# Softmax normalisation and phase wrapping on GpSimd, a split closing sum and new instruction orders in a one-core token-fusion kernel

## The chip, the cores and the metric

One Trainium2 chip, one of its cores. The time is the device time of one launch in microseconds (us); the median of several runs counts. The engines are PE (TensorE, matrix products, with its weight loads PEld), DVE (VectorE), ACT (ScalarE), POOL (GpSimd) and SP (SyncE, which issues most transfers). Each has its own queue of instructions and works through it in order; they wait for each other by semaphores only.

## The reference

Sixteen images and sixteen texts go through three layers. All arithmetic is fp32.

```python
# 1. tokens of an image: 2x2 convolution of stride 2 -> 144 tokens of 64, one attention without heads
feat = conv(x, conv_w) + conv_b                        # reshaped to (16, 144, 64)
Q, K, V = feat @ wq.T + bq, feat @ wk.T + bk, feat @ wv.T + bv
h = softmax(Q @ K.T / 8) @ V @ wo.T + bo
h = concatenate([h, txt], axis=1)                      # (16, 272, 64)
# 2. a phase memory on layernorm(h), added to h
n = layernorm(h)
pos = (cumsum(v1 * cos(p)) * cos(p) + cumsum(v1 * sin(p)) * sin(p)) / sqrt(t)   # p = base_phases, v1 = n @ Wvp + bvp
kp, qp = pi * tanh(tanh(n @ Wk1 + bk1) @ Wk2 + bk2), pi * tanh(tanh(n @ Wq1 + bq1) @ Wq2 + bq2)
content = (causal memory of cos/sin(kp) with n @ Wvc + bvc, read by cos/sin(qp)) / sqrt(32 t)
g = softmax(relu(n @ Wg1 + bg1) @ Wg2 + bg2)
h = h + n + (layernorm(g0 * pos + g1 * content) * ln_g + ln_b) @ Wo + bo
# 3. eight experts on layernorm(h), the best two of each token, added to h
n = layernorm(h)
w = softmax over the two largest of n @ Wg + bg, zero elsewhere
h = h + sum_e w[e] * (gelu(n @ W1[e] + b1[e]) @ W2[e] + b2[e])
```

## The kernel before

**Tiles.** The 64 features lie on the partitions, two images at a time (64 + 64 = 128), so sixteen images are eight pairs of 272 columns each. Layers 1 and 2 run over pairs (0 to 7); everything that goes token by token (layer norms, gates, routing, experts) runs over five groups of 3, 4, 4, 3 and 3 windows of 128 columns (`GW`, groups 0 to 4).

**Stages.** A stage is a name with an index, such as `exps:3`. For a pair: `taps` (DVE, the convolution, three sets of pairs), `qk` (PE, then `qkv` on DVE and `keys` on ACT copy the result out), `scores` (PE, then the row maximum on DVE), `exps` (ACT, four exponentials with their row sums, L585), `probs_n` (DVE, reciprocal and one multiplication, L817 and L819), `probs_t` (PE transposes, ACT copies), `mix` (PE, ACT). Then `h0_t` and `ln1_stats`/`ln1_norm` for a group (DVE; the power -1/2 comes from POOL, L484, the `root` helper), `residual` (POOL, L503 and L506), and for a pair `hidden`, `phases`, `phase_abs`, `trig`, `memory`, `recall`, `content`, and `streams` (DVE running sum, then POOL L511 and L512). A group goes on with `combine`, `ln2_stats`, `norm_s`, `attn_out`, `ln3_stats`, `ln3_norm`, `xn2_t`, `route`, `weights_t`, `wide` (transfers that spread the routing weights), sixteen `expert` products (PE, gelu on ACT, L697), eight `expert_out` products (PE L1236; DVE multiplies by the weight, L952; POOL adds up, L523) and `finish` (PE transposes the sum back, L1208, DVE adds it to `res`, L958, SP stores).

**Once only.** `base` takes the base phases into (-pi, pi] with six DVE instructions on 128x272 (L786 to L791), then ACT takes sines (L563 to L566), which needs another table than the exponentials, and POOL multiplies. `ln2_w` folds the layer norm's scale and bias into a weight: it waits for the transfer of `attw` (L657, L658 on ACT; L1176, L1177 on PE).

**What sets the order.** Each engine runs through a list of stages written out in `PLAN`; a stage waits for its inputs and for its PSUM bank, and all that stands behind it on that engine waits too. `BANKS` gives each stage its bank. `spare:n` in PE's list puts n matmuls on a matrix of ones into the bank that the next stage takes, behind that bank's last reader:

```python
                for _ in range(spare.pop() if spare else 0):
                    pe.matmul(ps[:, bank, 0:128], ones[:, 0:128], ones[:, 0:128], start=True, stop=True)
```

Of the kernel before, what the change touches and what calls it, by code (L numbers as in the profile page):

```python
# [139 lines left out]
phases:2 content:3 content:4 mix_gate:2 recall:0 gate_z:2 h0_t:4 memory:1 hidden:3 hidden:4 memory:2 phases:3  # L140
phases:4 recall:1 xn_t:3 xn_t:4 combine:0 content:5 mix_gate:3 memory:3 content:6 norm_s:0 content:7
mix_gate:4 attn_out:0 hidden:5 hidden:6 hidden:7 phases:5 phases:6 gate_z:3 gate_z:4 memory:4 values:2
phases:7 recall:2 recall:3 memory:5 memory:6 recall:4 recall:5 xn2_t:0 values:3 values:4 route:0 expert:0
memory:7 expert:1 logit_t:0 values:5 expert:2 expert:3 expert:4 combine:1 expert_out:0 expert_out:1 recall:6
combine:2 recall:7 norm_s:1 expert:5 weights_t:0 attn_out:1 norm_s:2 expert:6 expert_out:2 expert:7 attn_out:2
expert:8 expert_out:3 expert:9 values:6 values:7 expert:10 expert_out:4 xn2_t:1 expert:11 route:1 expert:12
expert:13 logit_t:1 expert_out:5 expert_out:6 expert:14 expert:15 spare:1 expert:16 expert_out:7 weights_t:1
combine:3 xn2_t:2 expert:17 route:2 expert:18 expert:19 norm_s:3 logit_t:2 expert:20 expert:21 expert:22
expert:23 attn_out:3 expert_out:8 expert_out:9 expert_out:10 expert_out:11 weights_t:2 expert:24 expert:25
# [1176 lines left out]
```

## Time and profile before

| | |
|---|---|
| median of 3 runs | 248.57 us (248.51 to 248.88) |
| the profiled execution | 249.06 us, of which 247.3 us from its first to its last instruction |
| granted TensorE clock, mean | 0.979 of full speed |
| busy share of the span | PE 91%, DVE 68%, ACT 60%, PEld 52%, POOL 41% |
| chain that ended last | PE 54%, DVE 23%, issue 9%, ACT 5%, SP's queue 4%, POOL 2% |

The busy shares are means over stages with different limits; a stretch is read by the engine that is busy nearly all of it. The chain is followed back from the last instruction, at each step to what released it.

### The profile page before, as it was taken

To read this page: it belongs to the slowest core of one execution; us is meant where nothing else is said; L and a number is where in the kernel's file an instruction comes from. 1 tells how busy PE (TensorE), PEld (TensorE's weight loads), DVE (VectorE), ACT (ScalarE), POOL (GpSimd) and SP (SyncE) were. 2 spreads that over 40 slices of the span, in tenths; PEclk is the share of its full clock that TensorE was granted. 3 is DMA by queue.
4 is the path that set the end of the run, shared out by engine and by line. 5 is a ranking of instruction groups with operands and counts; after the bars stand their busy time and mean duration, and the time that the engine had idled before them with its cause. 6 is when DMAs were issued, how large, how long until landed. Compare 5 with 4: busy or idle time off the path is not lost.

```text
span 247.3 us, 4625 instructions
## 1 busy us (share of the span) xinstructions
PE 226.0 (91%) x1546; PEld 128.0 (52%) x1546; DVE 167.1 (68%) x485; ACT 148.0 (60%) x300; POOL 102.1 (41%) x93
## 2 busy tenths in 40 slices
PE   7689799698889999999978999998999999999991
PEld 5578577475776765644324433542433445445440
DVE  2779587999999999999999791849023553213121
ACT  4677978885674775344546806592843655673640
POOL 3000233778852529156865253415146043333333
PEclk9959999999999999999999999999999999999997
DMA  7671000000000000026000933920900025601001
GB/s 187 140 252 67 0 3 0 0 3 0 5 0 3 0 3 0 3 71 189 1 0 19 243 86 96 243 42 7 248 6 0 0 48 144 158 1 32 0 3 32
DMA packets 15239, 14.42 MB, mean 58 GB/s; under 512 B 8528, under 2 KB 13680, under 8 KB 15088
## 3 DMA queue, kind: packets, MB, share of 16 engines
q1 hardware_dynamic: 14640, 13.66, 21.8%
q10 hardware_dynamic: 576, 0.47, 0.7%
q8 instruction: 13, 0.21, 0.4%
q14 instruction: 10, 0.08, 0.1%
HBM read 12.87 MB, written 1.25 MB: 57 GB/s over the span
## 4 chain that ended last, share of the span: by engine, by line
PE 54%; DVE 23%; issue 9%; ACT 5%; SPq 4%; POOL 2%; DMA 1%; POOLq 0%; ACTq 0%; DVEq 0%
PE ps L1223 22%; PE ps L1236 17%; ACT arena L585 3%; DVE stat L747 3%; DVE trig L862 2%; DVE scaled L952 2%; DVE y L852 2%; PE ps L1169 2%; DVE xn L771 1%; DVE k L780 1%; DVE vc L842 1%; SPq L411 1%; PE ps L973 1%; DMA attw<-in_attw 1%; PE ps L1011 1%
## 5 line engine op out<-in xcount | busy, mean ns | idle before, releaser
L697 ACT ACTIVATE arena<-ps,cols 128x768 f32<-128x768 f32 (+1 forms) x80 | 73.5, 990 | 30.6 <-PE ps L1223 26.3
L1223 PE MATMUL ps<-xt,w 64*128 64x384 f32 (+1 forms) x320 | 66.2, 544 | 0.2 <-DVE mem L872 0.2
L523 POOL TENSOR_TENSOR acc<-acc,scaled 128x384 f32<-128x384 f32 (+1 forms) x35 | 40.3, 1153 | 55.7 <-DVE scaled L952 54.8
L1236 PE MATMUL ps<-arena,w 128*64 128x384 f32 (+1 forms) x320 | 62.1, 534 | 0.5 <-DVE scaled L952 0.5
L952 DVE SCALAR_TENSOR_TENSOR scaled<-ps,b_col,wide 128x384 f32<-128x384 f32 (+1 forms) x35 | 23.2, 669 | 48.2 <-PE ps L1236 48.1
L484 POOL TENSOR_TENSOR rstd<-vare,minus_half 128x6 f32<-128x6 f32 (+1 forms) x15 | 24.8, 1652 | 46.3 <-DVE vare L756 46.1
L1223 PEld LDWEIGHTS ps<-xt,w 64*128 64x128 f32 x320 | 28.9, 186 | 26.3 <-issue 10.8
L1236 PEld LDWEIGHTS ps<-arena,w 128*64 128x64 f32 x320 | 21.5, 136 | 37.0 <-issue 29.2
L511 POOL TENSOR_TENSOR cum<-cum,turn_n 128x544 f32<-128x544 f32 x8 | 11.2, 1398 | 9.6 <-DVE cum L856 9.6
L721 DVE SCALAR_TENSOR_TENSOR arena<-arena,cols 128x108 f32<-128x108 f32 (+1 forms) x36 | 9.2, 312 | 5.3 <-ACT arena L550 5.1
L585 ACT ACTIVATE arena<-ps,negmax 72x144 f32<-72x144 f32 x32 | 11.6, 375 | 1.0 <-DVE negmax L812 1.0
L611 ACT ACTIVATE xt<-ps 128x256 f32<-128x256 f32 (+1 forms) x20 | 6.0, 350 | 10.1 <-PE ps L1064 10.1
L856 DVE TENSOR_TENSOR_SCAN cum<-ones,y 128x544 f32<-128x544 f32 x8 | 11.7, 1456 | 0.3
L492 POOL TENSOR_TENSOR turn_n<-turn_p,phase 128x544 f32<-128x544 f32 x1 | 1.3, 1333 | 24.1 <-ACT turn_p L566 24.1
L747 DVE BATCH_NORM_STATS2 stat<-res 128x6 f32<-128x64 f32 x68 | 9.5, 210 | 0.2
L973 PE MATMUL ps<-ones 128*128 128x128 f32 x28 | 4.5, 293 | 5.4 <-ACT arena L572 2.5
L1130 PE MATMUL ps<-trig 64*128 64x272 f32 (+2 forms) x96 | 8.5, 308 | 0.9 <-ACT trig L641 0.9
L1130 PEld LDWEIGHTS ps<-trig 64*128 64x128 f32 x96 | 7.8, 186 | 2.5 <-issue 1.3
L512 POOL TENSOR_TENSOR h0s<-cum 128x272 f32<-128x272 f32 x8 | 8.4, 1051 | 0.6
L872 DVE TENSOR_TENSOR mem<-ps,mask 128x864 f32<-128x864 f32 x8 | 8.3, 1043 | 0.2
L1141 PE MATMUL ps<-mem,vc 128*64 128x272 f32 (+2 forms) x96 | 7.6, 297 | 0.7 <-DVE mem L872 0.7
L771 DVE SCALAR_TENSOR_TENSOR xn<-xn,rstd 128x384 f32<-128x384 f32 (+1 forms) x10 | 8.1, 811 | 0.2
(158 smaller groups left out, 365.0 us busy)
## 6 DMA issues: line engine op xcount, KB each, us to landing
wide<-rows_of SPq DMA_DIRECT2D x24, 192.0 KB, 4.1
wide<-rows_of SPq DMA_DIRECT2D x16, 256.0 KB, 6.0
w<-in_w SPq DMA_DIRECT2D x1, 1024.0 KB, 5.2
out<-res SPq DMA_DIRECT2D x6, 96.0 KB, 1.9
h0s<-in_txt SPq DMA_DIRECT2D x1, 512.0 KB, 5.9
w<-in_w SPq DMA_DIRECT2D x1, 512.0 KB, 6.0
out<-res SPq DMA_DIRECT2D x4, 128.0 KB, 3.3
arena<-in_x_a SPq DMA_DIRECT2D x2, 144.0 KB, 3.6
```

The lines of the kernel that those rows point to most:

```text
L484: pool.tensor_tensor(rstd[:, kind, g % 2, 0:nb(g)], vare[:, kind, g % 2, 0:nb(g)], minus_half[:, 0:nb(g)], ALU.pow).then_inc(rstd_ok[kind], 1)
L511: link(pool.tensor_tensor(cum[:, i % 2, :, :], cum[:, i % 2, :, :], turn_n[:, :, :], ALU.mult))
L523: pool.tensor_tensor(acc[:, g % 2, 0:128 * GW[g]], acc[:, g % 2, 0:128 * GW[g]], scaled[:, i % 2, 0:128 * GW[g]], ALU.add).then_inc(S["acc ...
L585: ins = act.activation(probs[0:SC, i % 2, k, :], ps[0:SC, bank("scores", i) + k // 2, SI * (k % 2):SI * (k % 2) + SI], ACT.Exp, bias=negma ...
L697: act.activation(hidden_e[:, i % HIDDEN, 0:2 * n].rearrange("p (h t) -> p h t", h=2), ps[:, b:b + 2, 0:n], ACT.Gelu, bias=col("b1", 2 * e ...
L747: ins = dve.bn_stats(stat[:, g % 2, k, :], src[:, 64 * k:64 * k + 64])
L771: return dve.scalar_tensor_tensor(out=blocks(dst[:, 0:64 * n]), in0=blocks(dst[:, 0:64 * n]), scalar=8.0, in1=spread(rstd[:, kind, g % 2, ...
L856: dve.tensor_tensor_scan(cum[:, i % 2, :, :].rearrange("p k t -> p (k t)"), ones[:, :], y[:, i % 2, :, :].rearrange("p k t -> p (k t)"), 0 ...
L952: dve.scalar_tensor_tensor(out=total, in0=ps[:, bank("expert_out", i), 0:n], scalar=b2_col[:, e:e + 1], in1=wide[:, g % 2, e, 0:n], op0=AL ...
L1130: ins = pe.matmul(ps[:, bank("memory", i) + h, MOFF[k]:MOFF[k] + L - q], trig[r, 0, L * i + m:L * i + m + 128], trig[r, 1, L * i + q:L * i ...
L1223: ins = pe.matmul(ps[:, bank("expert", i) + h, 0:n], w1[r, c:c + 128], xt[r, GC[g]:GC[g] + n], start=True, stop=True)
L1236: ins = pe.matmul(ps[64 * h:64 * h + 64, bank("expert_out", i), 0:n], w2[:, 2 * (i % E) + j, :], hidden_e[:, (2 * i + j) % HIDDEN, n * h:n ...
```

## The change

Five edits and new lists:

1. `probs_n`: DVE keeps the reciprocal; the multiplication of 72x576 goes to POOL, in a stage of POOL's list, and PE's `probs_t` waits for it there.
2. `base`: the wrapping goes from DVE to POOL as a stage `reduce:0`, nine instructions for six, since each multiply-and-add becomes two. ACT's `base:0` stands early, ahead of `keys:2` and the first `exps`.
3. `spare`: three matmuls in one place, in bank 5, which no stage ahead of it uses, and without a wait; before, fourteen in five places.
4. `ln2_w` stands later on PE and ACT.
5. The last `expert_out` (index 39) is not added by POOL. DVE writes it in three pieces, and PE's `finish:4` turns back both the sum so far and the last piece into one bank (matmuls with the identity, the second adding to the first). ACT issues one of the last two stores. `attn_out` gets a buffer of its own (`ao` for `c2`).

```diff
+SPARE = [(3, 5)]
+CLOSING = (5, 2, 3)
...
-qk:0 qk:1 spare:3 scores:0 scores:1 ln2_w:0 qk:2 qk:3 val:0 probs_t:0 val:1 qk:4 scores:2 mix:0 val:2 qk:5
+qk:0 qk:1 spare:0 scores:0 scores:1 val:0 val:1 qk:2 qk:3 qk:4 ln2_w:0 probs_t:0 scores:2 probs_t:1 mix:0 qk:5
...
+                if stage == "probs_n":
+                    pool.wait_ge(S["rowinv"], i + 1)
+                    pool.tensor_tensor(probs[0:SC, i % 2, :, :], probs[0:SC, i % 2, :, :],
+                                       rinv[0:SC, i % 2, :].unsqueeze(2).to_broadcast([SC, 4, SI]), ALU.mult)\
+                        .then_inc(S["pnorm"], 1)
+                elif stage == "reduce":
+                    pool.wait_ge(ld["phase"], 16)
+                    raw = phase[:, 0, :]
+                    link(pool.tensor_scalar(turns[:, :], raw, float(1 / (2 * np.pi)), ROUND, ALU.mult, ALU.add))
+                    link(pool.tensor_scalar(turns[:, :], turns[:, :], ROUND, None, ALU.subtract))
+                    for part in (TWO_PI_1, TWO_PI_2, TWO_PI_3):
+                        link(pool.tensor_scalar(turn_n[:, 0, :], turns[:, :], part, None, ALU.mult))
+                        link(pool.tensor_tensor(raw, raw, turn_n[:, 0, :], ALU.subtract))
+                    pool.tensor_scalar(raw, raw, PI32, -PI32, ALU.min, ALU.max).then_inc(S["reduced"], 1)
...
-                elif stage == "expert_out" and i % E > 0:
+                elif stage == "expert_out" and 0 < i % E and i < E * NG - 1:
...
+            act.wait_ge(S["out_sb"], NG)
+            act.dma_start(*store_of(NG - 1, 1)).then_inc(S["stored"], 16)
...
+                    if i >= 2:
+                        dve.wait_ge(S["pnorm"], i - 1)
                     dve.reciprocal(rinv[0:SC, i % 2, :], rsum[0:SC, i % 2, :]).then_inc(S["rowinv"], 1)
-                    dve.wait_ge(S["rowinv"], i + 1)
-                    dve.tensor_tensor(probs[0:SC, i % 2, :, :], probs[0:SC, i % 2, :, :],
...
+                    if i == E * NG - 1:
+                        for w in range(GW[g]):
+                            c = slice(128 * w, 128 * w + 128)
+                            dve.scalar_tensor_tensor(out=total[:, c], in0=ps[:, bank("expert_out", i), c], scalar=b2_col[:, e:e + 1],
+                                                     in1=wide[:, g % 2, e, c], op0=ALU.add, op1=ALU.mult).then_inc(S["last_sb"], 1)
...
+                    if i == NG - 1:
+                        pe.wait_ge(S["acc_sb"], added(i, E - 2))
+                        last = (E * NG - 1) % 2
+                        for w in range(GW[i]):
+                            take(CLOSING[w], "out_sb", NG)
+                            pe.matmul(ps[:, CLOSING[w], 0:128], acc[:, i % 2, 128 * w:128 * w + 128], ident[:, :],
+                                      start=True, stop=False)
+                        for w in range(GW[i]):
+                            pe.wait_ge(S["last_sb"], w + 1)
+                            pe.matmul(ps[:, CLOSING[w], 0:128], scaled[:, last, 128 * w:128 * w + 128], ident[:, :],
+                                      start=False, stop=True).then_inc(S["last_mm"], 1)
```

Where the lists differ, three places matter for the prediction. In these rows a name is the tile written, then the tiles read, with the shape of the output; `arena` holds all of layer 1, `ps` is PSUM, `cols` and `rows` are parameters. First **ACT's queue in the opening**, from `keys:0` on, before:

```order
L572 ACTIVATE arena<-ps,cols 128x144 x2
L557 ACTIVATE wvo<-ps 128x128
L558 ACTIVATE bvo<-ps,cols 128x1
L657 ACTIVATE scaled_wo<-attw,cols 128x128
L658 ACTIVATE ln_b_w<-ones,cols 128x128
L585 ACTIVATE arena,rsum<-ps,negmax 72x144 x4
```

and now:

```order
L593 ACTIVATE arena<-ps,cols 128x144 x2
L578 ACTIVATE wvo<-ps 128x128
L579 ACTIVATE bvo<-ps,cols 128x1
L557 ACT_TABLE_LOAD
L584 ACTIVATE turn_p<-phase 128x272
L585 ACTIVATE turns<-phase 128x272
L587 ACTIVATE turn_p<-turns,cols 128x272
L593 ACTIVATE arena<-ps,cols 128x144
L557 ACT_TABLE_LOAD
L606 ACTIVATE arena,rsum<-ps,negmax 72x144 x4
L678 ACTIVATE scaled_wo<-attw,cols 128x128
```

The sines with their two table loads and `keys:2` now stand ahead of the first exponentials, and the norm fold behind them.

Second **POOL's queue in layer 1 and the start of layer 2** (`cum` is the running sum of `streams`, `rstd` the power -1/2), before:

```order
L492 TENSOR_TENSOR turn_n<-turn_p,phase 128x544
L484 TENSOR_TENSOR rstd<-vare,minus_half 128x6
L500 TENSOR_TENSOR out_row<-out_row,rows 128x64
L503 TENSOR_TENSOR res<-res,out_row 128x384
L506 TENSOR_TENSOR res<-res,xn 128x384
L484 TENSOR_TENSOR rstd<-vare,minus_half 128x8
L503 TENSOR_TENSOR res<-res,out_row 128x512
L506 TENSOR_TENSOR res<-res,xn 128x512
L484 TENSOR_TENSOR rstd<-vare,minus_half 128x8
```

and now, behind the nine instructions of `reduce:0`:

```order
L513 TENSOR_TENSOR turn_n<-turn_p,phase 128x544
L497 TENSOR_TENSOR arena<-arena,rinv 72x576 x4
L491 TENSOR_TENSOR rstd<-vare,minus_half 128x6
L521 TENSOR_TENSOR out_row<-out_row,rows 128x64
L524 TENSOR_TENSOR res<-res,out_row 128x384
L527 TENSOR_TENSOR res<-res,xn 128x384
L497 TENSOR_TENSOR arena<-arena,rinv 72x576 x2
L491 TENSOR_TENSOR rstd<-vare,minus_half 128x8
L497 TENSOR_TENSOR arena<-arena,rinv 72x576
L524 TENSOR_TENSOR res<-res,out_row 128x512
L527 TENSOR_TENSOR res<-res,xn 128x512
L497 TENSOR_TENSOR arena<-arena,rinv 72x576
```

The eight multiplications (L497) stand among the powers and the residual sums; the power for group 2 is the next row.

Third **PE's last rows**, before:

```order
L1236 MATMUL ps<-arena,w 64x384 x8
L1223 MATMUL ps<-xt,w 128x384 x10
L1236 MATMUL ps<-arena,w 64x384 x16
L1208 MATMUL ps<-ident,acc 128x128 x3
L218 UNCONDITIONAL_BRANCH
```

and now:

```order
L1278 MATMUL ps<-arena,w 64x384 x4
L1265 MATMUL ps<-xt,w 128x384 x10
L1278 MATMUL ps<-arena,w 64x384 x20
L1250 MATMUL ps<-ident,acc 128x128 x3
L1241 MATMUL ps<-ident,acc 128x128 x3
L1245 MATMUL ps<-ident,scaled 128x128 x3
L220 UNCONDITIONAL_BRANCH
```

`finish:3` (the first three on `acc`) has come to the end too, ahead of the six matmuls of `finish:4`.

## Rows read from the trace of the kernel before

**Rows 1.** Busy us by stretch: length, then PE, PEld, DVE, ACT, POOL, granted clock.

```profile
10.00:20.00 10.00, 8.06 (x54) 7.52 (x54) 7.56 (x24) 6.36 (x30) 0.00 (x0) 0.66 0.60 199
...
30.00:40.00 10.00, 8.41 (x81) 6.68 (x81) 6.92 (x22) 8.52 (x37) 4.20 (x4) 1.00 0.01 2
40.00:50.00 10.00, 7.94 (x86) 5.59 (x85) 9.51 (x38) 8.16 (x31) 5.61 (x4) 1.00 0.00 0
50.00:60.00 10.00, 9.22 (x90) 6.61 (x87) 9.82 (x23) 7.41 (x16) 7.51 (x6) 1.00 0.01 2
60.00:70.00 10.00, 8.23 (x97) 6.63 (x95) 9.79 (x24) 6.77 (x15) 8.17 (x7) 1.00 0.01 3
...
120.00:130.00 10.00, 8.13 (x44) 3.13 (x40) 9.52 (x23) 4.41 (x6) 7.84 (x6) 1.00 0.00 1
...
160.00:180.00 20.00, 19.12 (x92) 7.85 (x90) 9.77 (x36) 13.80 (x18) 5.54 (x4) 1.00 0.43 102
```

**Rows 2.** Timeline: start, duration in us, engine, line; brackets: idle before, its releaser.

```profile
9.79 2.01 DVE L721 SCALAR_TENSOR_TENSOR arena<-arena,cols 128x108 f32<-128x108 f32 x8
...
14.05 0.40 ACT L657 ACTIVATE scaled_wo<-attw,cols 128x128 f32<-128x128 f32 x1 [2.79 <-DMA attw<-in_attw]
...
14.65 0.36 ACT L585 ACTIVATE arena<-ps,negmax 72x144 f32<-72x144 f32 x1
...
40.15 0.62 ACT L605 ACTIVATE res<-ps 128x512 f32<-128x512 f32 x1
```

**Rows 3.** Timeline of ACT around the sines of the base phases.

```profile
24.78 1.28 ACT L536 ACT_TABLE_LOAD   x1
...
26.86 0.52 ACT L566 ACTIVATE turn_p<-turns,cols 128x272 f32<-128x272 f32 x1
...
28.20 1.28 ACT L536 ACT_TABLE_LOAD   x1
```

**Rows 4.** Groups by line and shape: count, busy us, mean ns, idle before.

```profile
L511 POOL TENSOR_TENSOR cum<-cum,turn_n 128x544 f32<-128x544 f32 x8 | 11.2, 1398 | 9.6 <-DVE cum L856 9.6
...
L512 POOL TENSOR_TENSOR h0s<-cum 128x272 f32<-128x272 f32 x8 | 8.4, 1051 | 0.6
...
L819 DVE TENSOR_TENSOR arena<-arena,rinv 72x576 f32<-72x576 f32 x8 | 7.3, 912 | 0.3
...
L721 DVE SCALAR_TENSOR_TENSOR arena<-arena,cols 128x108 f32<-128x108 f32 x24 | 6.4, 324 | 0.8 <-ACT arena L550 0.7
...
L789 DVE SCALAR_TENSOR_TENSOR phase<-turns,phase 128x272 f32<-128x272 f32 x3 | 1.3, 442 | 0.1
```

**Rows 5.** Transfers: issues, KB each, median us from issue to landing.

```profile
out<-res SPq DMA_DIRECT2D x6, 96.0 KB, 1.9
...
phase<-in_phase ACTq DMA_DIRECT2D x1, 272.0 KB, 4.2
```

**Rows 6.** Timeline of POOL and DVE in the end of layer 1.

```profile
45.61 1.27 POOL L503 TENSOR_TENSOR res<-res,out_row 128x512 f32<-128x512 f32 x1 [0.81 <-DVE xn L771]
...
45.78 1.72 DVE L819 TENSOR_TENSOR arena<-arena,rinv 72x576 f32<-72x576 f32 x1
...
50.01 0.75 DVE L819 TENSOR_TENSOR arena<-arena,rinv 72x576 f32<-72x576 f32 x1
```

**Rows 7.** Timeline of PE at the routing weights of group 1.

```profile
130.25 0.27 PE L1197 MATMUL ps<-ident,wsp 128*64 128x128 f32 x1 [1.22 <-DVE wsp L933]
```

**Rows 8.** Timeline of the end, behind the last expert product.

```profile
241.55 0.62 DVE L952 SCALAR_TENSOR_TENSOR scaled<-ps,b_col,wide 128x384 f32<-128x384 f32 x1 [0.67 <-PE ps L1236]
242.25 0.99 POOL L523 TENSOR_TENSOR acc<-acc,scaled 128x384 f32<-128x384 f32 x1 [0.29 <-DVE scaled L952]
...
243.39 0.52 PE L1208 MATMUL ps<-ident,acc 128*128 128x128 f32 x3 [1.88 <-POOL acc L523]
243.94 0.56 DVE L958 TENSOR_TENSOR res<-ps,res 128x384 f32<-128x384 f32 x1 [1.77 <-PE ps L1208]
244.53 0.90 SPq L455 DMA_DIRECT2D out<-res  x2
```

More of the change, by code:

```diff
@@ L140 @@
[L140 to L149, printed above, removed]
@@ L150 @@
-expert:26 expert:27 expert_out:12 expert_out:13 xn2_t:3 finish:0 combine:4 route:3 expert:28 expert:29
-norm_s:4 logit_t:3 expert:30 expert:31 expert:32 expert:33 expert:34 expert:35 expert:36 attn_out:4
-weights_t:3 expert_out:14 expert_out:15 expert_out:16 xn2_t:4 expert:37 expert:38 expert:39 expert:40
-expert:41 expert:42 expert:43 expert_out:17 expert_out:18 expert_out:19 expert_out:20 expert_out:21 route:4
-expert:44 expert:45 expert:46 expert:47 expert:48 expert:49 logit_t:4 finish:1 expert_out:22 expert_out:23
@@ new lines @@
+mix_gate:2 memory:0 gate_z:2 phases:2 phases:3 h0_t:4 recall:0 memory:1 hidden:4 memory:2 memory:3 phases:4
+recall:1 xn_t:3 values:2 xn_t:4 combine:0 mix_gate:3 content:5 content:6 content:7 mix_gate:4 hidden:5
+hidden:6 gate_z:3 norm_s:0 gate_z:4 phases:5 phases:6 attn_out:0 hidden:7 recall:2 recall:3 phases:7 memory:4
+memory:5 memory:6 values:3 values:4 recall:4 memory:7 xn2_t:0 recall:5 route:0 expert:0 expert:1 logit_t:0
+expert:2 recall:6 combine:1 expert:3 expert:4 expert_out:0 expert_out:1 norm_s:1 values:5 weights_t:0 expert:5
@@ new lines @@
+attn_out:1 expert:6 expert:7 expert_out:2 expert_out:3 expert:8 combine:2 recall:7 expert:9 expert:10 values:6
+expert:11 norm_s:2 xn2_t:1 expert_out:4 route:1 expert:12 logit_t:1 attn_out:2 expert_out:5 expert:13
+expert:14 combine:3 expert_out:6 expert:15 expert:16 weights_t:1 values:7 expert_out:7 norm_s:3 expert:17
+attn_out:3 expert:18 expert:19 expert:20 expert_out:8 expert_out:9 xn2_t:2 expert:21 expert:22 expert:23
+expert_out:10 expert_out:11 route:2 expert:24 expert:25 expert:26 logit_t:2 expert:27 expert_out:12
@@ new lines @@
+expert_out:13 xn2_t:3 weights_t:2 finish:0 combine:4 route:3 expert:28 expert:29 norm_s:4 logit_t:3 expert:30
+expert:31 expert:32 expert:33 expert:34 expert:35 expert:36 expert:37 weights_t:3 attn_out:4 expert_out:14
+expert_out:15 expert_out:16 expert_out:17 expert_out:18 xn2_t:4 expert:38 expert:39 expert:40 expert:41
+expert:42 expert:43 expert_out:19 expert_out:20 expert_out:21 route:4 expert:44 expert:45 expert:46 expert:47
+expert:48 expert:49 logit_t:4 expert_out:22 expert_out:23 expert_out:24 weights_t:4 finish:1 expert:50
@@ L178 @@
[L178 to L179 removed]
+taps:0 taps:1 taps:2 taps:3 qkv:0 qkv:1 taps:4 taps:5 scores:0 scores:1 qkv:2 taps:6 qkv:3 taps:7 qkv:4 taps:8
+gate_w:0 probs_n:0 probs_n:1 scores:2 qkv:5 probs_n:2 scores:3 qkv:6 probs_n:3 ln1_stats:0 scores:4 ln1_norm:0
+qkv:7 scores:5 probs_n:4 probs_n:5 ln1_stats:1 scores:6 gate_p:0 scores:7 content:0 ln1_norm:1 probs_n:6
+streams:0 probs_n:7 ln1_stats:2 phase_abs:0 content:1 gate_p:1 ln1_norm:2 content:2 streams:1 ln1_stats:3
@@ L180 @@
+expert_out:26 expert_out:27 expert_out:28 expert_out:29 expert_out:30 finish:2 expert_out:31 expert_out:32
+expert_out:33 expert_out:34 expert_out:35 expert_out:36 expert_out:37 expert_out:38 expert_out:39 finish:3
+finish:4
 """),
     "act": order("""
-tap0:0 fold_t:0 tap0:1 tap0:2 keys:0 keys:1 fold:0 ln2_w:0 exps:0 ln2_wc:0 exps:1 keys:2 keys:3 probs_t:0
-val:0 val:1 keys:4 mix:0 val:2 exps:2 keys:5 probs_t:1 base:0 mix:1 probs_t:2 exps:3 h0_t:0 keys:6 mix:2 val:3
-val:4 val:5 val:6 probs_t:3 exps:4 mix:3 val:7 xn_t:0 exps:5 probs_t:4 gate_h:0 keys:7 h0_t:1 mix:4 probs_t:5
@@ L971, in take @@
                 reader[bank] = (S[read_out], count)
-                for _ in range(spare.pop() if spare else 0):
-                    pe.matmul(ps[:, bank, 0:128], ones[:, 0:128], ones[:, 0:128], start=True, stop=True)
             wq, wk, wo, wv = (tokw[:, 128 * k:128 * k + 128] for k in range(4))
@@ L997, in _ @@
                 if stage == "spare":
-                    spare.append(i)
+                    n, b = SPARE[i]
+                    if b in reader:
+                        pe.wait_ge(*reader[b])
+                    for _ in range(n):
+                        pe.matmul(ps[:, b, 0:128], ones[:, 0:128], ones[:, 0:128], start=True, stop=True)
                 elif stage == "qk":
```

183 lines of the change are left out of this document (91 added, 92 removed), and 8 rows, old and new, of the table BANKS.

## Prediction

> **What bounds the kernel now.** I read the busy time by stretch first [rows 1]. From 40 us on DVE is busy 9.5 to 9.8 of every 10 us, so it bounds layer 2. In the stretch 30 to 40 it is busy only 6.9 of 10 and ACT 8.5: there ACT and the way round between the engines bound layer 1. In 160 to 180 PE is busy 19.1 of 20 while DVE is at half: PE bounds the experts. POOL is nobody's bound by its share of the span, but in 60 to 70 it is busy 8.2 of 10 beside a full DVE. Then I read the opening [rows 2, 3]: ACT waits 2.79 us for `attw` and starts its first exponentials at 14.65; later it spends 24.78 to 29.48 on two table loads of 1.28 and three sines, a `mix` and a `probs_t` copy among them. The end [rows 8] is a chain without overlap: last product, DVE, POOL, PE, DVE, stores.
>
> So a microsecond counts in full where DVE is saturated, where ACT is (up to `h0_t:1`, which ends at 40.15 + 0.62 = 40.77), where PE idles among the experts, and in the closing chain.
>
> **Opening and layer 1 (edits 1 to 4).** Removed from ACT between 24.8 and 29.5: two table loads and the sines, which fill 26.06 to 27.38 [rows 3], so 2 x 1.28 + 1.32 = 3.9 us of a nearly full engine. They move ahead of the first `exps`, into the time in which ACT waited for `attw`, which waits no more there. What they cost is set by POOL's nine instructions of `reduce:0`. The phases land at about 2.2 + 4.2 = 6.4 [rows 5], the issue being the last of ACT's four. No row shows POOL at this work with one operand. From below I take DVE's own 0.44 for 128x272, from above POOL's 1.05 for two operands of that size, blocked times included [rows 4]: 4.0 to 9.5 us in all. Two thirds read one operand, so I take 0.75 each, 6.8 us: done at 13.2. ACT comes to the table load at 14.05 - 2.79 = 11.3 [rows 2] and has it by 12.6. The sines then end at 13.2 + 1.3 = 14.5, `keys:2` 0.4 later, and after another table load the exponentials start at 16.2, against 14.65.
>
> `keys:2` hangs on the convolution's second set, whose last eight taps end at 11.80 [rows 2]. Each tap reads two SBUF operands, and that POOL holds up such a DVE instruction is in the trace: the multiplication that started at 45.78 beside POOL's 1.27 took 1.72 us, the one at 50.01 took 0.75 [rows 6]. If four or five of the nine instructions fall ahead of a tap, 4.5 x 0.75 = 3.4 us, the taps end at 15.2; product, copy and table load behind them take about 2.4 (an estimate, 1.7 of it the copy and the load), so the exponentials start at about 17.6. Between 15.7 (short instructions, no collisions) and 17.6 I take 16.9: 2.2 us late, against 3.9 gained.
>
> The Trainium skill (SBUF — State Buffer, "Who interferes with whom") says that a DVE instruction with two SBUF inputs contends with a GpSimd instruction that reads SBUF and that the later one waits for all of the other. The 1.72 against 0.75 agrees. By that rule the sum would take the end of 17.6 and not 16.9, 0.7 us more.
>
> The eight multiplications cost 0.91 each on DVE. On POOL I price them at the 1.40 of 128x544 [rows 4], as no row has 72x576 there. Six of them ran in layer 1, where DVE has 3 us of 10 free [rows 1]: nothing is won there, and the way from exponentials to transposes grows by 0.5 plus a hand-over. PE waits at `probs_t`, and behind it on PE stand the next pair's `scores` and the `mix` whose copies ACT is to make. The pairs are double-buffered, so ACT's other copies cover most of it; uncovered, six times 0.6 would be 3.6 us; I take 0.7. `ln2_w` is on the path to nothing before the first `attn_out`: nothing. Eleven spare matmuls go from places where PE waited or had room: nothing by themselves. They kept PE busy, though: the granted clock of 10 to 20 is 0.66 [rows 1], a part of it at 1.2 for 2.4 GHz, after PE had stood idle. Such a stretch once more, in layer 1 where ACT bounds, I bound by 0 and 1 us and take none.
>
> Sum of this part: -3.9 + 2.2 + 0.7 = **-1.0 us** (-3 to +1).
>
> **Layer 2 (edit 1).** The last two multiplications lay in the saturated stretch: 1.72 + 0.75 = 2.5 us off DVE's path [rows 6]. What is late next is POOL. In 40 to 60 it is busy 5.6 + 7.5 = 13.1 of 20 [rows 1]; with four of the multiplications, 5.6 us, it is at 18.7, before any holding up. In its queue `probs_n:7` stands behind `residual:1` and ahead of the power of group 2, for which DVE's `ln1_norm:2` waits; behind that instruction the whole of DVE's list waits. Counted from the exponentials of pair 7 this power ends some 2 us after DVE comes to it. In 60 to 70 POOL has only 1.8 us of 10 to catch up. I take 1.5 us of such waits (0 to 5): **-1.0 us** (-2.5 to +2.5).
>
> **Experts (lists, and the spare at group 1's weights).** PE idles 10 - 8.13 = 1.9 us in 120 to 130 and 0.9 in 160 to 180 [rows 1]; the largest piece is the 1.22 at the routing weights [rows 7]. Between `logit_t:1` and `weights_t:1` the old list has two `expert_out`, three `expert` and a spare matmul; the new one has `attn_out:2`, `combine:3`, two `expert_out` and four `expert`, so I count that wait as covered. Between `attn_out:4` and `xn2_t:4` stand five `expert_out` for three. At most 2.8 us can go; the routing weights of group 1 get less time to be spread before their first use, which can cost up to 1.5. I take **-1.0 us** (-2.8 to +1.5).
>
> **The end (edit 5).** Before, from the last product's end at 241.5 to the last instruction at 247.3: 5.8 us [rows 8]. Now DVE writes three pieces; from the 0.32 of 128x108 [rows 4] I take 0.3 each: the last at +0.95. `finish:3`'s transposes (0.5) lie beside that. The sum without the last product comes from POOL: DVE's writes follow each other by 0.67 + 0.62 = 1.3, so the addition before the last ended 1.3 ahead of 243.24, at 241.9, +0.4; the six matmuls take about twice 0.5, to +1.5. DVE now does `finish:3` first (0.56, to +1.55), then three pieces of 0.25: +2.3, against 244.50, +3.0, before. The stores: two issues took 0.90 on SP; now one on each of SP and ACT, but SP has the two of `store:3` just before, so the last issue ends near +2.9, and with 1.9 to land [rows 5] the end is at +4.8. **-1.0 us** (-1.4 if `store:3` is out of the way, -0.3 if its transfers and these share the engines).
>
> **Sum.** -1.0 - 1.0 - 1.0 - 1.0 = -4.0. The profiled execution took 249.06, so 245.06; it lies 0.49 above the median of 248.57, so I forecast **244.6 us**.
>
> **Rivals.**
> *Everything that is covered stays covered*: exponentials at 15.7, no waiting for POOL, all but one of the idle microseconds gone, and the short end: -2.8 - 2.5 - 1.5 - 1.2 = -8.0: 240.6. For it speaks that POOL is empty up to 27 us and that the lists were made anew with these edits; against it POOL's load from 40 on.
> *The work is moved, not saved*: layer 1 ends when it did, POOL's waits take back the 2.5 us, PE's idle time goes elsewhere; only the end is shorter: 247.6. For it speaks that the three places are coupled: each engine there waits for another one.
> *POOL becomes the bound of layer 1's end* (the slower side): with collisions its 18.7 of 20 us is over 20, and the backlog cannot drain in 60 to 70. Then each of the powers of groups 2, 3 and 4 makes DVE wait, 1.8 us each: -2.5 + 5.4 = +2.9 in layer 2; the opening at its late end gives +0.5; experts 0, end -1.0: +2.4, so 251.0. With the other parts as forecast it decides from the point where DVE's waits for POOL between 45 and 75 us pass 5.5 us (1.0 + 2.5 + 1.0 + 1.0). The 8.2 of 10 in 60 to 70 speaks for it; against it, that `streams` is not urgent there.
> *Nothing*: an opening at its late end against the end's gain: 248.6.
>
> **How the numbers follow.** A measurement of this kernel can tell about 0.2% (0.5 us) from no change. Chances: the forecast 0.45 (its own range 243.0 to 246.6), all covered 0.15, moved 0.17, POOL the bound 0.18, nothing 0.05. Faster by over 0.2%: 0.45 + 0.15 + 0.17 = 0.77; within: 0.05; slower: 0.18. The range runs from 241.0, which leaves out half of "all covered", to 249.8, which leaves out two thirds of "POOL the bound": 0.08 + 0.12 = 0.2.
>
> **What would show it.** Right: the first exponentials (72x144) start between 15.7 and 17.6, `h0_t:1` ends a microsecond or more before 40.77, DVE in 40 to 60 shows waits for POOL's powers of 1 to 2 us in all, PE's wait at the weights of group 1 is gone, and 4.8 us pass from the last product to the end. Wrong: exponentials after 18.5 (collisions with the taps are dearer), DVE waiting for POOL over 5 us between 45 and 75, a second stretch at 1.2 GHz after 24 us, or multiplications on POOL far from 1.4 us.

## The result and the profile after

The changed kernel takes **256.44 us** (four runs, 255.46 to 258.04) beside 248.72 for the kernel before (four runs, 248.51 to 249.14): a ratio of 1.031 with an interval of 1.026 to 1.037. It is 3.1% slower; the forecast of 244.6 and its range up to 249.8 are both wrong. The profiled execution took 255.46 us, its span is 253.6, its mean granted clock 0.946 for 0.979. Ratios here leave disturbed runs out; where runs of one kernel differ by their granted clock, I give the clock beside the time.

The stretches of [rows 1], now with 20 to 30 us as well (length, then PE, PEld, DVE, ACT, POOL, granted clock, share and rate of the transfers):

```profile
10.00:20.00 10.00, 5.44 (x36) 3.91 (x36) 8.36 (x30) 7.15 (x22) 5.92 (x6) 0.79 0.57 199
20.00:30.00 10.00, 9.09 (x56) 6.87 (x56) 2.10 (x8) 6.42 (x27) 3.39 (x3) 0.50 0.01 3
30.00:40.00 10.00, 9.91 (x90) 8.31 (x86) 5.55 (x19) 7.21 (x28) 3.73 (x4) 0.85 0.00 0
40.00:50.00 10.00, 8.22 (x82) 5.85 (x80) 6.45 (x26) 8.95 (x39) 7.21 (x7) 1.00 0.01 2
50.00:60.00 10.00, 8.10 (x70) 5.73 (x70) 8.74 (x22) 7.62 (x17) 9.17 (x7) 0.84 0.01 2
60.00:70.00 10.00, 10.00 (x72) 6.38 (x74) 7.55 (x18) 4.18 (x9) 5.40 (x5) 0.65 0.00 1
120.00:130.00 10.00, 9.85 (x66) 5.14 (x65) 9.59 (x28) 5.04 (x9) 6.70 (x6) 1.00 0.00 0
```

Read the clock first. From 20 to 30 us it is 0.50, that is 1.2 GHz for the whole stretch, where the kernel before had 1.00 with this row:

```profile
20.00:30.00 10.00, 9.24 (x91) 7.19 (x90) 7.95 (x26) 8.94 (x25) 1.33 (x1) 1.00 0.01 3
```

PE is as busy as before (9.09 for 9.24) and gets 56 matmul records done for 91; DVE, which waits for it, falls from 7.95 to 2.10. The same happens again in 60 to 70: PE at 10.00, DVE at 7.55 where it was full. The mean clock of 0.946 over 253.6 us means 2 x 0.054 x 253.6 = 27 us at 1.2 GHz.

What PE did before the clock fell: its timeline in the opening and in 54 to 57 us (start, duration, idle before and its releaser in brackets; one fp32 product leaves two records, x2).

```profile
13.75 0.51 PE L1031 MATMUL ps<-arena,tokw 128*128 128x144 f32 x2 [0.56 <-DVE arena L812]
14.99 0.51 PE L1033 MATMUL ps<-arena,tokw 128*128 128x144 f32 x2 [0.73 <-DVE arena L812]
16.59 0.85 PE L1031 MATMUL ps<-arena,tokw 128*128 128x144 f32 x2 [1.08 <-ACT arena L593]
17.90 0.85 PE L1033 MATMUL ps<-arena,tokw 128*128 128x144 f32 x2 [0.46 <-DVE arena L812]
20.30 0.80 PE L1205 MATMUL ps<-scaled_wo,centre 128*128 128x128 f32 x2 [1.56 <-ACT arena L593]
...
54.10 0.69 PE L1061 MATMUL ps<-ident,arena 72*72 72x72 f32 x8 [0.49 <-POOL arena L497]
...
56.46 0.62 PE L1082 MATMUL ps<-ident,h0s 128*128 128x128 f32 x3 [0.95 <-DVE vc L855]
```

The single products last 0.51 at 14.99 and 0.85 at 16.59: the clock fell between them, after waits of 0.56, 0.73 and 1.08 us with a single product between each two (`qk:3` now has both its products in bank 6, `qk:4` in bank 7, so each waits for the copy of the one before; the 1.08 ends with ACT's `keys:2`, which edit 2 put behind the sines). The second fall is at about 57 us, behind waits of 0.49 and 0.95.

The opening on ACT and POOL, which the prediction had at 13.2 (end of `reduce:0`) and 16.9 (first exponentials):

```profile
13.77 1.17 POOL L508 TENSOR_SCALAR phase<-phase 128x272 f32<-128x272 f32 x1
...
14.97 0.43 ACT L584 ACTIVATE turn_p<-phase 128x272 f32<-128x272 f32 x1 [2.77 <-POOL phase L508]
...
16.55 1.28 ACT L557 ACT_TABLE_LOAD   x1
17.85 0.38 ACT L606 ACTIVATE arena<-ps,negmax 72x144 f32<-72x144 f32 x1
...
42.40 0.62 ACT L626 ACTIVATE res<-ps 128x512 f32<-128x512 f32 x1
```

`h0_t:1` ends at 43.02 for 40.77 [rows 2]. In layer 2 the first `combine` of DVE starts at 82.50, the first gelu at 99.69 for 92.00, the last product's DVE work at 248.49 for 241.55 [rows 8]. So about 2 us are lost by the end of `h0_t:1` and 5 more by the first gelu (7.7 in all); behind it 0.7 come back (6.9 at the last product).

### The profile page after: what moved, and what is told of

Its sections match the earlier page's. It is cut to its first block, busy times and chain, and to the rows that moved or that the text cites. A ratio compares the mean times of both kernels' runs of the same rounds, so it can differ in the third digit from the quotient of the medians.

```text
span 253.6 us, 4613 instructions
## 1 busy us (share of the span) xinstructions
PE 233.7 (92%) x1533; PEld 130.8 (52%) x1533; DVE 163.3 (64%) x475; ACT 148.9 (59%) x300; POOL 115.1 (45%) x109
## 4 chain that ended last, share of the span: by engine, by line
PE 55%; DVE 25%; issue 9%; POOL 7%; ACT 2%; DMA 1%; ACTq 0%; DVEq 0%; POOLq 0%
PE ps L1265 18%; PE ps L1278 16%; DVE stat L771 3%; PE ps L1136 2%; DVE scaled L973 2%; PE ps L1072 2%; DVE y L865 2%; PE ps L1120 2%; DVE cum L869 2%; PE ps L1159 2%; DMA phase<-in_phase 1%; PE ps L1170 1%; POOL rstd L491 1%; PE ps L1051 1%; PE ps L1061 1%
## 5 line engine op out<-in xcount | busy, mean ns | idle before, releaser
L544 POOL TENSOR_TENSOR acc<-acc,scaled 128x384 f32<-128x384 f32 (+1 forms) x34 | 38.9, 1143 | 58.0 <-DVE scaled L973 57.5
L973 DVE SCALAR_TENSOR_TENSOR scaled<-ps,b_col,wide 128x384 f32<-128x384 f32 (+1 forms) x34 | 22.6, 670 | 43.1 <-PE ps L1278 42.5
L1265 PEld LDWEIGHTS ps<-xt,w 64*128 64x128 f32 x320 | 28.9, 186 | 27.1 <-issue 11.8
L497 POOL TENSOR_TENSOR arena<-arena,rinv 72x576 f32<-72x576 f32 x8 | 9.1, 1143 | 13.7 <-DVE rinv L834 13.7
L745 DVE SCALAR_TENSOR_TENSOR arena<-arena,cols 128x108 f32<-128x108 f32 (+1 forms) x36 | 10.0, 340 | 4.8 <-ACT arena L571 4.7
L827 DVE TENSOR_REDUCE negmax<-ps 72x4 f32<-72x576 f32 x8 | 5.9, 747 | 5.1 <-PE ps L1051 5.0
L1061 PE MATMUL ps<-ident,arena 72*72 72x72 f32 x64 | 6.5, 253 | 2.4 <-POOL arena L497 2.4
L651 ACT ACTIVATE hid<-ps,cols 128x544 f32<-128x544 f32 x8 | 5.6, 712 | 4.7 <-PE ps L1120 4.7
```

The lines of the kernel that those rows point to most:

```text
L544: pool.tensor_tensor(acc[:, g % 2, 0:128 * GW[g]], acc[:, g % 2, 0:128 * GW[g]], scaled[:, i % 2, 0:128 * GW[g]], ALU.add).then_inc(S["acc ...
L745: dve.scalar_tensor_tensor(out=o, in0=pix[:, tap, a:b, :], scalar=col("conv_w", 4 * c + tap), in1=o, op0=ALU.mult, op1=ALU.add).then_inc(S ...
L973: dve.scalar_tensor_tensor(out=total, in0=ps[:, bank("expert_out", i), 0:n], scalar=b2_col[:, e:e + 1], in1=wide[:, g % 2, e, 0:n], op0=AL ...
L1265: ins = pe.matmul(ps[:, bank("expert", i) + h, 0:n], w1[r, c:c + 128], xt[r, GC[g]:GC[g] + n], start=True, stop=True)
```

## Experiments

**The theories.** Theory 1: without the spare matmuls, and with longer waits of PE, the granted clock falls twice, and that is most of the loss. Theory 2: POOL's queue, and the sines ahead of the exponentials, cost it. Theory 3: the new banks (the table `BANKS` is new too) and orders make PE wait.

**PE's pauses of the changed kernel filled.** `e1_keepwarm` (here and below, of the lists only the pieces that differ):

```diff
+HOLD = {(3, 0): 2, (3, 1): 2, (4, 0): 4, (4, 1): 2}
...
+                    hold(HOLD.get((i, 0), 0), 5, 384)
                     take(bank("qk", i), "q_sb", i + 1)
...
+qk:4 hold:0 ln2_w:0
...
+hold:2 probs_t:7 content:2 hold:3 h0_t:3
```

> The kernel after, with fourteen more matmuls on the ones (128 columns each) put where PE stands idle ahead of the two stretches at 1.2 GHz (granted clock 0.50 from 15.9 to 32.9 us and from 56.8 to 67 us in the trace of after): ten at qk:3, qk:4 and ln2_w, six at probs_t:7 and h0_t:3. Nothing else is changed. Theory 1 (the clock: PE's pauses, no longer filled, let it fall twice, and the half clock is most of the loss): both stretches shrink or go, combine:0, now at 82.5, comes 4 to 9 us earlier, and the time is 247.5 to 252.5. Theory 2 (POOL's work and the sines ahead of the first exponentials are the loss): the clock may rise but the time stays at 254.5 to 257. Theory 3 (the new banks and orders make PE wait for copies, and the clock only follows from that): 254 to 257 as well, with the same waits at qk:3, qk:4 and ln2_w.

(Counted in the code it is 21 matmuls, fifteen and six, not fourteen.) The median of 255.23 us lies in the range of theories 2 and 3 and not in that of theory 1. What tells them apart is the spread: ten runs went from 248.07 us at a granted clock of 0.999 and 248.92 at 1.00, over 252.77 at 0.98 and 255.26 at 0.966, to 260.57 at 0.933. The instructions are the same in all of them, and 12.5 us lie between the ends: the size that theory 1 needs is there, and theories 2 and 3 name nothing that changes from run to run. But this filling does not hold the clock. In the profiled run (257.43 us) PE waits 2.16 us for POOL at `probs_t:0` and 1.33 at `probs_t:4`. So, filled further (36 matmuls, not the 27 of the text), `e11_after_filled`:

```diff
+HOLDS = [(5, 5, 384), (5, 6, 0), (5, 2, 0), (0, 4, 0), (4, 4, 0), (4, 4, 0)]
...
+hold:0 ln2_w:0 hold:1 probs_t:0
...
+mix_gate:0 hold:2 probs_t:4
...
+hold:4 probs_t:7 content:2 hold:5 h0_t:3
```

> The kernel after with the same 27 matmuls on the ones, in more of PE's pauses than the fourteen of e1_keepwarm (there the runs went from 248.07 us at a granted clock of 0.999 to 260.57 at 0.933). Theory 1: with the longest pauses (2.16 us at probs_t:0 and 1.33 at probs_t:4 in the trace of e1_keepwarm) filled the clock is held more often: 247.5 to 251, most runs over 0.985. Theories 2 and 3, and the possibility that the clock falls whatever fills PE: 253 to 257.

Ten runs, 248.94 to 250.18, all at 0.999 or 1.00; median **249.37**, ratio to before 1.003 (1.001 to 1.005). Its stretches, to be read against those of after:

```profile
10.00:20.00 10.00, 8.74 (x76) 7.98 (x76) 9.89 (x32) 7.95 (x25) 5.47 (x6) 1.00 0.61 201
20.00:30.00 10.00, 9.01 (x94) 7.48 (x93) 3.32 (x10) 7.89 (x36) 3.65 (x4) 1.00 0.00 2
...
60.00:70.00 10.00, 8.83 (x100) 6.47 (x98) 9.79 (x32) 6.32 (x13) 6.69 (x6) 1.00 0.01 2
```

94 matmul records for 56 in 20 to 30, and DVE full again in 60 to 70. The clock therefore costs the changed kernel 256.44 - 249.37 = **7.1 us**, about 0.26 us for each of the 27 at 1.2 GHz. It may be more, since the 249.37 holds whatever the 36 matmuls cost: the two runs of `e1_keepwarm` at 0.999 and 1.00, with 21 of them, took 248.07 and 248.92, on another chip than `e11_after_filled`, which makes it 7.5 to 8.4. And the clock is not the whole miss. The kernel before has three runs at a clock of 1.00 among those beside the experiments, 247.65 to 247.80 us, so with the full clock on both sides the change still costs 0.3 to 1.7 us, where -4.0 was forecast.

**The spare matmuls alone.** `e2_before_cold` takes all fourteen out of the kernel before, `e5_first_three` the eleven that the change took out:

```diff
-probs_t:1 spare:3 mix:1
+probs_t:1 mix:1
...
-val:5 spare:5 val:6
+val:5 val:6
...
-values:0 spare:2 xn_t:1
+values:0 xn_t:1
...
-expert:15 spare:1 expert:16
+expert:15 expert:16
```

> The kernel before without its fourteen matmuls on the ones; nothing else is changed. Theory 1 (the spare matmuls hold the clock): a longer first stretch at 1.2 GHz than 11.9 to 18.6 us and perhaps a second one behind 24 us; 250 to 255 us. Theories 2 and 3 (POOL; banks and orders), and the step of the prediction that called the removal of eleven of them nothing: the clock as before and 248.2 to 249.2 us.

> The kernel before with edit 3 alone: of the fourteen matmuls on the ones the first three stay, the eleven at mix:1, val:6, xn_t:1 and expert:16 go. Theory 1 (the spare matmuls hold the clock): a stretch at 1.2 GHz behind 24 us, as in the kernel before without any, and 250.5 to 254 us. The prediction's step (nothing by themselves) and theories 2 and 3: granted clock as before, 248.2 to 249.2 us.

253.82 us (ratio 1.020, 1.018 to 1.023) and 252.54 (1.015, 1.012 to 1.019). Everything else is the kernel before, yet stretches at 1.2 GHz lie behind 30 us, where the profile before has none: `e2_before_cold` is at 0.66 in 30 to 40 and 0.50 in 50 to 60, and of `e5_first_three`, whose opening (10 to 30) is at 1.00, these are the rows:

```profile
30.00:40.00 10.00, 9.14 (x79) 7.23 (x79) 7.91 (x23) 8.33 (x34) 4.21 (x4) 0.83 0.01 2
40.00:50.00 10.00, 7.75 (x77) 4.87 (x76) 9.56 (x39) 7.51 (x29) 6.29 (x4) 0.90 0.00 0
50.00:60.00 10.00, 10.00 (x51) 7.74 (x51) 6.79 (x21) 6.05 (x11) 6.13 (x6) 0.50 0.01 2
```

Both medians lie in the ranges of theory 1. The prediction's "nothing by themselves" is false by 3.6 us.

**One edit undone.** `e3_wrap_on_dve` (edit 2) and `e4_norm_on_dve` (edit 1), each with the lists' entries put back:

```diff
-reduce:0 base:0 probs_n:0 probs_n:1 probs_n:2 probs_n:3 ln1_stats:0
+probs_n:0 probs_n:1 probs_n:2 base:0 probs_n:3 ln1_stats:0
-gate_w:0 probs_n:0 probs_n:1 scores:2 qkv:5
+gate_w:0 probs_n:0 probs_n:1 scores:2 base:0 qkv:5
```
```diff
-                    if i >= 2:
-                        dve.wait_ge(S["pnorm"], i - 1)
                     dve.reciprocal(rinv[0:SC, i % 2, :], rsum[0:SC, i % 2, :]).then_inc(S["rowinv"], 1)
+                    dve.wait_ge(S["rowinv"], i + 1)
+                    dve.tensor_tensor(probs[0:SC, i % 2, :, :], probs[0:SC, i % 2, :, :],
```

> The kernel after with edit 2 undone: the phases are wrapped by DVE's six instructions behind scores:2, ACT's sines stand behind mix:1 again and POOL's product behind probs_n:2. Theory 2: the first exponentials start at 14.5 to 15.7 for 17.85, and 2 to 4 us are won: 252.5 to 254.5. Theory 1: PE's pause ahead of the exponentials is 2 to 3 us shorter; if the clock stays up for that the time is 249 to 253, and if it falls all the same the sines' 3.9 us on ACT come back into layer 1 and it is 255 to 258. Theory 3: waits at bank 7 and bank 6 are unchanged, 255 to 258.

> The kernel after with edit 1 undone: the eight multiplications of the probabilities are DVE's again, and POOL's list is without them. Theory 2: PE waits for POOL's product no more (2.4 us in after) and the way from exponentials to transposes is shorter; 252.5 to 254.5. Theory 1: the first stretch at 1.2 GHz stays; the second may go, since PE's pause of 0.49 us at 54.1 waited for POOL: 250 to 253 if it goes and 255 to 257 if it stays. Theory 3: 255 to 257.5, DVE having 6 to 7 us more to do.

255.31 (1.027) and 253.38 us (1.020). The first exponentials of `e3_wrap_on_dve` start at 13.41 for 17.85 and this gains 1 us only: its clock is 0.52 in 20 to 30 and 0.71 in 40 to 50, so 0.952 over the launch; PE waits 3.22 us for POOL's multiplication ahead of `probs_t:0`, up to 19.96. `e4_norm_on_dve` ran at 0.966 in three runs out of four; its median lies in the range of theory 2 and in neither of theory 1's. Neither undoing brings the clock back, so neither edit alone is the cause of its fall.

**One edit alone, on the kernel before.**

> The kernel before with edit 1 alone: the eight multiplications of the probabilities on POOL, put into its list at the places of after; banks, spares and the other lists stay. The prediction's terms for it, +0.7 in layer 1 and -1.0 in layer 2, give 248.3 (247.3 to 249.5). Theory 2 (POOL's normalisation is dear): 250 to 252, at a granted clock as before. Theory 1: by itself nothing; where PE's longer wait at probs_t lets the clock fall the time is 251 to 255, and the fall is seen in the windows. Theory 3: 248 to 249, as the banks are the old ones.

> The kernel before with edit 2 alone: nine instructions on POOL wrap the phases, and ACT's sines stand ahead of ln2_w and the first exponentials. The prediction's terms for it, -3.9 and +2.2, give 246.9 (245.5 to 248.5), if the clock is as before. Theory 2 (POOL's late reduce and the sines delay the exponentials more than they save): first exponentials at 17 to 18.5 and 249 to 251 at a granted clock as before. Theory 1: PE's longer pause ahead of the exponentials gives a longer first stretch at 1.2 GHz or one more, and 249 to 254. Theory 3: 246 to 248, as the banks are the old ones.

> The kernel before with edit 5 alone (without the extra buffer of attn_out): three pieces of the last product, the sum closed on PE, one of the last stores on ACT. The prediction's term, -1.0, gives 247.6; the trace of after shows 5.16 us from the last product to the end for 5.8, so 248.0. All three theories: 247.4 to 248.3, granted clock as before. Over 248.6 the closing turn itself would be at fault.

The edits are those shown in the diff of the change, with `probs_n` or `reduce` put into POOL's list and, for edit 2, `base:0` ahead of `ln2_w:0` on ACT. Edit 1: 250.68 us at a clock of 0.995, 252.93 at 0.977, 254.03 at 0.964, 255.39 at 0.971. Edit 2: 250.15 at 0.988, and 253.70 to 254.54 at 0.950 to 0.958. Both lose without any loss of spares, above the ranges that the prediction's terms gave (up to 249.5 and 248.5), and most runs of both lose the clock: the clock of the kernel before is held narrowly. PE's wait in each, ahead of `probs_t:4` and ahead of `ln2_w`:

```profile
40.26 0.80 PE L1036 MATMUL ps<-ident,arena 72*72 72x72 f32 x8 [1.67 <-POOL arena L491]
```
```profile
17.77 0.77 PE L1176 MATMUL ps<-scaled_wo,centre 128*128 128x128 f32 x2 [5.23 <-ACT ln_b_w L667]
```

Edit 5 alone: 248.40 us beside 248.97 for before, ratio 0.997 (0.995 to 0.9994), clock mostly 0.993; the expected range ended at 248.3. A gain of 0.6 us by the medians and of 0.7 by its trace (5.06 us from the last product's end at 242.04 to the span's end, for 5.8).

**A version that beats both, and the measure at full clock.** `e9_tail_fill` is the kernel before with edit 5 and sixteen matmuls without a wait in the opening:

```diff
-qk:0 qk:1 spare:3 scores:0 scores:1 ln2_w:0 qk:2
+qk:0 qk:1 fill:8 spare:3 scores:0 scores:1 fill:8 ln2_w:0 qk:2
...
+                if stage == "fill":
+                    for _ in range(i):
+                        pe.matmul(ps[:, 7, 0:128], ones[:, 0:128], ones[:, 0:128], start=True, stop=True)
```

> The kernel before with edit 5 and, in the opening, sixteen more matmuls on the ones in a bank that is free there (bank 7), without a wait: eight ahead of the spares at scores:0 and eight ahead of ln2_w, where the trace of before shows PE idle for 2.22 and 1.20 us. Theory 1: the first stretch at 1.2 GHz (11.9 to 18.6 us in before, 0.98 to 0.993 over the launch) goes, the granted clock is 0.995 or more in every run, and the time is 246.3 to 247.5. Theories 2 and 3 (the clock follows, it does not lead): 247.8 to 248.6, as with edit 5 alone.

**247.09 us**, ratio 0.9946 (0.9915 to 0.9978). Eight of twelve runs lie at 246.74 to 247.20 with a clock of 1.00, four at 250.33 to 250.78 with 0.971 or 0.972: the expected "every run" failed, since the clock still falls in a third of them. What the sixteen matmuls buy is runs at the full clock: `e8_tail_alone`, without them, has two such runs in twelve, at 247.07 and 247.38. Its row of the opening, for 8.06 and 0.66 in [rows 1]:

```profile
10.00:20.00 10.00, 9.89 (x92) 8.21 (x91) 8.42 (x28) 6.57 (x31) 0.00 (x0) 1.00 0.58 201
```

**Edits 1 and 2 at full clock.** On this kernel each is put alone, with PE's new wait filled too (`hold:6 probs_t:4`; `fill:18` for `fill:8` ahead of `ln2_w:0`):

> The kernel e9_tail_fill (247.09 us; 246.74 to 247.20 at a granted clock of 1.00) with edit 1 and six more matmuls on the ones ahead of probs_t:4, where the trace of e6_norm_alone shows PE waiting 1.67 us for POOL. If edit 1 has a price of its own at full clock (theory 2; e6_norm_alone took 250.68 us at a clock of 0.995): 249 to 250.5 at a clock of 0.99 or more. If its whole price was the clock (theory 1): 246.5 to 247.6. The prediction's terms, +0.7 and -1.0: 246.8.

> The kernel e9_tail_fill with edit 2 and eighteen for eight matmuls on the ones ahead of ln2_w, where the trace of e7_wrap_alone shows PE waiting 5.23 us for ACT. The prediction's terms, -3.9 for ACT and +2.2 for later exponentials: 245.4. If its price at full clock is that of the later exponentials (theory 2; e7_wrap_alone had them at 18.93 and took 250.15 us at a clock of 0.988): 247.5 to 249.5. If its whole price was the clock (theory 1): 245.0 to 247.2.

In the runs at 0.999 or 1.00, `e12_fill_norm` takes 249.51 to 249.90 (five of ten) and `e13_fill_wrap` 249.41 to 249.90 (four of ten), for 246.74 to 247.20: **+2.7 us for either edit** with the clock held, in which the six and ten further matmuls are counted too, and for edit 2 also that `ln2_w` stands where it stood (PE waits 5.23 us for it in `e7_wrap_alone`; edit 4 moves it). The rest of their runs, 250.91 to 253.62, are at 0.972 to 0.986. Theory 2 holds here, as the smaller part. For edit 1, DVE and POOL in `e12_fill_norm` (its profiled run is at 1.00 up to 40 us):

```profile
35.85 0.18 DVE L833 RECIPROCAL rinv<-rsum 72x4 f32<-72x4 f32 x1 [0.20 <-ACT arena L596]
...
36.59 0.99 POOL L517 TENSOR_TENSOR res<-res,xn 128x384 f32<-128x384 f32 x1
37.55 2.25 POOL L496 TENSOR_TENSOR arena<-arena,rinv 72x576 f32<-72x576 f32 x2
38.25 0.17 DVE L833 RECIPROCAL rinv<-rsum 72x4 f32<-72x4 f32 x1 [2.23 <-ACT arena L596]
```

The reciprocal of pair 4 is done at 36.03, but the multiplication stands behind `residual:0` in POOL's queue and starts at 37.55, 1.5 us later. `h0_t:1`'s copy comes at 40.54 for 38.51 in `e9_tail_fill`; 0.56 of these 2.03 us are older, as its first exponentials start at 14.60 for 14.04, behind the transfer of `attw`.

**What is left: banks and orders.** `e10_lists_alone` has edits 1 and 2 both undone and the filling of `e11_after_filled`:

> The kernel after with edits 1 and 2 undone (multiplication and wrapping on DVE, the sines behind mix:1) and with 27 matmuls on the ones in PE's pauses of the opening, at probs_t:0, probs_t:4, probs_t:7 and h0_t:3: what is left of the change is the new banks and orders, the later norm fold and edit 5. Theory 3 (banks and orders are the loss): 252 to 256 though the clock is held. Theory 1: granted clock 0.98 or more and 246.5 to 249. Theory 2: 246.5 to 249 as well, whatever the clock does.

251.91 us at 0.993, 254.09 at 0.986, 256.20 and 257.27 at 0.973 and 0.967 (36 matmuls here too). The ranges of theories 1 and 2 failed. The median, 255.14, lies in theory 3's, but the clock was not held, and the run nearest to the full clock lies just below that range. The trace shows one place of the loss:

```profile
28.45 0.85 PE L1057 MATMUL ps<-arena,tokw 128*128 128x144 f32 x2 [2.14 <-ACT arena L595]
```

PE waits for `keys:5`, which in this kernel stands behind the sines I had put back behind `mix:1`. With edits 1 and 2 in place the same lists take 249.4 (`e11_after_filled`), +2.4 at full clock, which is 2.7 + 2.7 - 2.4 = 3.0 us less than the two edits' prices added to `e9_tail_fill` would give. So, if the two prices add up, the new lists belong to the edits: with them they recover some 3 us of the 5.4, and without them they are a loss here, how much of it by the wait above and how much by the banks these runs do not tell. Distinct banks for `qk:3` and `qk:4` were not tried.

## Why the prediction was wrong

In steps from the kernel before to after, by medians: edit 5, -0.6 (`e8_tail_alone`); holding the clock, -1.3 (`e9_tail_fill`), which before does in few runs; edits 1 to 4 with the new lists at full clock, +2.3 (`e11_after_filled`, with what its 36 matmuls cost); the clock lost, +7.1. The sum is 7.5, measured were 7.7. Seen from the forecast, 256.44 is 11.8 us over 244.6: 7.1 of it is the clock, and 4.8 (249.37 less 244.6) is what the four terms of -1.0 lacked.

**The clock: the step that failed.** The prediction saw that the eleven matmuls kept PE busy, read 0.66 in [rows 1] as a stretch at 1.2 GHz after PE had stood idle, then bounded one more such stretch by 0 and 1 us and took none. There are two, of 17 and 10 us, and they cost 7.1. The bound was too small by its nature: at 1.2 GHz PE is on the path of layer 1 and of layer 2, where the rows of before from 30 us on, all at full clock, showed ACT and DVE as the bounds: in 60 to 70 of after PE is busy 10.00 of 10. A bound from the row at hand would have been the whole of layer 1 at half clock. "A second stretch at 1.2 GHz after 24 us" stood among the signs that would prove it wrong, and it was the one that came.

**The opening and layer 1 (-1.0).** Right in sign at full clock, by terms that were each off. `reduce:0` ended at 14.94 for 13.2, nine instructions of 0.51 to 1.17 for 0.75. The taps' second set was held up by far less than 3.4 us; in after its last eight

```profile
9.42 2.67 DVE L745 SCALAR_TENSOR_TENSOR arena<-arena,cols 128x108 f32<-128x108 f32 x8
```

end at 12.09, not 15.2 (11.80 before [rows 2]); they take 2.67 us for 2.01. POOL's instructions beside them took 0.90 to 1.07 where its first took 0.51, so it was rather POOL that waited, though the records do not show such a wait by itself. The rule on the shared port in the Trainium skill (SBUF — State Buffer, "Who interferes with whom") makes whichever comes later wait, and agrees with these rows only if that was mostly POOL. The prediction's own pair of rows was not clean either. The multiplication at 50.01 [rows 6], its undisturbed one at 0.75 us, ran beside POOL's power, which started before it and ended at 51.40:

```profile
49.37 2.03 POOL L484 TENSOR_TENSOR rstd<-vare,minus_half 128x8 f32<-128x8 f32 x1 [0.74 <-DVE vare L756]
```

So not every POOL instruction holds such a DVE instruction up for its whole length. At full clock the exponentials of `e11_after_filled` start at 17.11 for 14.04 in `e9_tail_fill`, +3.1 for the forecast +2.2, and `h0_t:1`'s copy at 38.17 for 38.51: so 3.4 us were won in between, near the 3.9 less 0.7 of the sum. Net -0.3 for -1.0, and -2.0 against the 40.15 of [rows 2]. In after itself the low clock turned this into +2.3.

**Layer 2 (-1.0).** Wrong in sign. The feared mechanism did not come: DVE waits for POOL's powers 0.7 us in all, not 1.5, and the rival "POOL the bound", which needed 5.5, is out. Normalisation on POOL was even cheaper than priced:

```profile
L497 POOL TENSOR_TENSOR arena<-arena,rinv 72x576 f32<-72x576 f32 x8 | 9.1, 1143 | 13.7 <-DVE rinv L834 13.7
```

1.14 for 1.40. What costs is the way round that I had called covered: exponentials, reciprocal, POOL's queue, transposes. At full clock edit 1 alone costs 2.7, not 0.7 - 1.0. Between `e9_tail_fill` and `e11_after_filled` the spans differ by 2.8 (247.7 and 244.9); less -0.3 for the opening and +1.0 for the experts, this leaves +2.1 for layer 2.

**The experts (-1.0).** Wrong. The 1.22 us at the weights of group 1 [rows 7] are gone, but 0.58 each stand now at the weights of groups 2 and 4 (163.36 and 206.58 us in after), and a wait of the same size stands ahead of `expert_out:6`, whose bank 1 `attn_out:2` still holds:

```profile
131.56 1.51 PE L1278 MATMUL ps<-arena,w 128*64 128x384 f32 x8 [1.29 <-DVE ao L908]
```

From 100 to 220 us at full clock PE is busy

```profile
100.00:220.00 120.00, 116.27 (x629) 51.48 (x630) 73.54 (x234) 66.44 (x89) 49.74 (x39) 1.00 0.33 83
```

in `e9_tail_fill` (old order), and

```profile
100.00:220.00 120.00, 115.33 (x626) 50.85 (x624) 77.85 (x237) 63.52 (x86) 52.03 (x41) 1.00 0.31 80
```

in `e11_after_filled` (new order): +0.9 us of idling, not -1.0. From the first gelu to the last product it is the same: 149.50 us with PE busy 145.56 in `e9_tail_fill`, 148.82 with 143.84 in `e11_after_filled`, so 3.9 and 5.0 of idling; the stage is 0.7 shorter only because 1.7 us of PE's work now lie outside it, above all `expert:1` (ahead of the first gelu) and `finish:3` (behind the last product), and a spare matmul is gone. That was the rival "moved, not saved", in this stage.

**The end (-1.0).** Right in its steps, a third too large. In after:

```profile
248.49 0.87 DVE L970 SCALAR_TENSOR_TENSOR scaled<-ps,b_col,wide 128x128 f32<-128x128 f32 x3 [0.67 <-PE ps L1278]
...
249.28 0.55 DVE L986 TENSOR_TENSOR res<-ps,res 128x384 f32<-128x384 f32 x1
...
249.85 1.46 SPq L462 DMA_DIRECT2D out<-res  x3
250.15 0.74 DVE L982 TENSOR_TENSOR res<-ps,res 128x128 f32<-128x128 f32 x3 [0.32 <-PE ps L1245]
250.92 0.47 ACTq L723 DMA_DIRECT2D out<-res  x1
```

DVE is done at +2.4 (forecast +2.3), the last issue ends at +2.9 (+2.9), the span at +5.1 for +4.8: the last transfer lands 2.2 us later, not 1.9. Alone the edit gives -0.7 by its trace and -0.6 by its times.

So of four terms two were right in sign and too large, two had the wrong sign, and the fifth, set to zero, was larger than all of them. With the clock held the kernel would have taken about 249.4: inside the range up to 249.8, but slower than before, which the forecast gave a chance of 0.18.
